# Router logits from extra columns of the attention's key and value matrices, score banks exponentiated from PSUM, and a large fill placed later

## The chip, the cores and the metric

The kernel runs on one core of one Trainium2 chip. The metric is the device time of one execution in microseconds (us). The kernel before was timed three times: 933.9, 938.02 and 944.68 us, median 938.02. Engines are named as in the profile: PE is TensorE (PEld its weight loads), DVE is VectorE, ACT is ScalarE, POOL is GpSimd, SP is SyncE, which here only starts DMAs.

## What is computed

A block with cross-attention and a mixture of nine experts, on 4 x 1024 tokens of 256 channels in float32. Layer norms, 16 heads of 64, 77 context rows per batch, two experts for each token:

```python
z = layernorm(layernorm(x)) ; c = layernorm(ctx)       # the second norm of each with weights and biases
q = (z @ Wq) * (1 + fside) + fside                     # 16 heads of 64
k, v = split(c @ Wkv)                                  # 77 rows for each batch
x = x + softmax(q @ k.T / 8) @ v @ Wout
h = layernorm(x)
logits = h @ Wr                                        # 9 experts; the top 2 of the softmax, weights w summing to 1
x = x + sum(w[e] * (silu(h @ Wg[e]) * (h @ Wu[e])) @ Wd[e] for e in top2)
```

The kernel never forms queries. For each batch it multiplies Wq into the keys (a *key matrix*, 256 x 16*77) and the values into Wout (a *value matrix*, 16*77 x 256). A token's scores are its normalised row times the key matrix, and the attention's output is its probabilities times the value matrix. Products that need full float32 accuracy are made from two float32r halves (hi, lo) in three matmuls (`product`, lines 224 to 231).

## The kernel before

**Stages.** Prepare (0 to about 74 us): the context is normalised, turned and multiplied by Wkv; Wq is mixed with the layer norm's weights; key and value matrices are made, and the value matrix goes through DRAM. Attention with routing (to about 389 us): T = 32 tiles of 128 tokens go through a software pipeline of T + 5 steps. Experts (408 us to the end): 40 tiles of 256 rows, gathered by expert, through gate, up and down products.

**The pipeline.** In step s, each engine runs its `step(s, c)`, an order written out by hand; engines meet only at semaphores. PE turns the probabilities of tile s-2 (line 996) in three groups, makes the router logits of tile s-4 (1020) from a transposed copy of the normalised row, makes the scores of tile s in three PSUM banks of 6, 6 and 4 heads, turns the next token rows (960) and the normalised rows of tile s-3 (964), makes the ranks of tile s-4 (1041, 1042), and multiplies probabilities by the value matrix (`attend`, tile s-2). DVE adds the attention of tile s-3 to the row, takes its statistics and normalises it, picks two experts for tile s-4 (`route`), inverts the sums of tile s-1 (`softmax_inv`), takes the minima of tile s and, for the first bank alone, subtracts them into SBUF (`softmax_in`, `DIRECT = 1`), and gives rows their slots (`allot`). ACT exponentiates the first bank of tile s-1 from SBUF and the other two of tile s straight from PSUM. POOL computes the reciprocal root of the variance, copies the row for the second expert (`make_rows`), multiplies the probabilities by the inverse sums (`divide`, 614), scatters two copies of the rows of tile s-5 to the experts' regions (`scatter`, 601, two indirect DMAs) and sums the gate's denominator of tile s-4 (`gate_sum`, 608). DVE's reciprocal of that sum (1352) is in its step between the probabilities' halves and `normalise`.

**Before the pipeline.** POOL fills `wq_head` (128 x 4096 elements, line 573) right after the root for the context's norm (572), while DVE normalises the context (1146). ACT later overwrites halves of `wq_head` with the mixed Wq. PE makes 8 pairs of key and value products, then the mixed Wq (929), then 32 key-matrix products (980) with 24 value products (947) between them.

## Time and profile before

| | us |
|---|---|
| median of three runs | 938.02 |
| the profiled execution's own time | 937.82 |
| its span, first to last instruction | 935.9 |
| prepare, until the first minimum of a score bank | 75.2 |
| attention and routing, until the ranks' last sum is read | 75.2 to 389.2 |
| gap until the experts' first matmul | to 408 |
| experts | 408 to 935.9 |
| PE, DVE, ACT, POOL busy | 865.1, 703.9, 650.7, 388.9 |

Busy times are sums over stages with different limits. Around the span lie 1.9 us in which no instruction runs. The chain of the work that ended last passes through PE for 67% of the span.

### The profile page before, as it was taken

What the parts mean: (1) busy time and instruction counts of PE and PEld (TensorE: products, weight loads), DVE (VectorE), ACT (ScalarE), POOL (GpSimd) and SP (SyncE); (2) the same over time, 40 slices, a digit from 0 to 9 for tenths busy, and PEclk for the clock granted to TensorE, in tenths of its full rate; (3) what the DMA queues carried; (4) which work ended last, traced back from release to release, by engine and by line L of the source; (5) the groups of instructions that cost most, each with busy time, mean ns of one, the idle gap of its engine ahead of it and who ended that gap; (6) DMA issues with size and microseconds to landing.
All of it is one profiled execution on the core that took longest, in us unless ns stands there. A gap on an engine that the chain in (4) does not pass through costs nothing.

```text
span 935.9 us, 22224 instructions
## 1 busy us (share of the span) xinstructions
PE 865.1 (92%) x6634; PEld 827.7 (88%) x6634; DVE 703.9 (75%) x1640; ACT 650.7 (70%) x2054; POOL 388.9 (42%) x475
## 2 busy tenths in 40 slices
PE   5997999999999998269999999999999999999993
PEld 4746999999999998259999999998999999999993
DVE  7766898888898786657876877776778777687771
ACT  3558888787888875247776777675767776677761
POOL 3001376676686666502343333333323433234332
PEclk9998999999999998769999999999999999999997
DMA  7158301310400207331225224355342254322222
GB/s 238 34 160 275 95 25 56 102 36 29 129 29 30 80 24 257 121 86 24 46 44 129 45 44 130 47 128 137 66 110 45 34 140 100 74 45 40 40 33 23
DMA packets 66681, 77.99 MB, mean 83 GB/s; under 512 B 7303, under 2 KB 58691, under 8 KB 66627
## 3 DMA queue, kind: packets, MB, share of 16 engines
q1 hardware_dynamic: 50947, 57.33, 20.6%
q0 software_dynamic: 14592, 18.95, 12.1%
q10 hardware_dynamic: 1088, 1.06, 0.4%
q8 instruction: 25, 0.41, 0.2%
q14 instruction: 29, 0.24, 0.1%
HBM read 113.46 MB, written 32.93 MB: 156 GB/s over the span
## 4 chain that ended last, share of the span: by engine, by line
PE 67%; DMA 11%; issue 7%; DVE 6%; SPq 4%; POOL 2%; ACT 2%; DVEq 1%; ACTq 0%; POOLq 0%
PE banks L229 19%; PE banks L230 18%; PE banks L231 18%; DMA wgt<-in_L_ffn_Wu 5%; PE banks L996 3%; DMA result<-res,tok_id 3%; PE banks L980 2%; PE banks L947 2%; PE banks L1099 1%; PE banks L1066 1%; PE banks L1020 1%; DVE hid_lo L1459 1%; DMA xs<-in_x 1%; POOL result L653 1%; PE banks L929 1%
## 5 line engine op out<-in xcount | busy, mean ns | idle before, releaser
L229 PE MATMUL banks<-tok_t_hi,wgt_hi 128*128 128x256 f32 x880 | 252.0, 286 | 9.6 <-DVE tok_t_lo L1428 9.5
L231 PE MATMUL banks<-tok_t_hi,wgt_lo 128*128 128x256 f32 x880 | 251.0, 285 | 0.0
L230 PE MATMUL banks<-tok_t_lo,wgt_hi 128*128 128x256 f32 x880 | 251.0, 285 | 0.0
L1440 DVE TENSOR_TENSOR wgt_lo<-wgt,wgt_hi 128x704 fp32r<-128x704 f32 (+1 forms) x240 | 207.6, 907 | 37.9 <-ACT wgt_hi L819 36.9
L653 POOL DMA_INDIRECT result<-res,tok_id x80 | 130.0, 1625 | 219.3 <-ACT res L846 191.5
L819 ACT ACTIVATE wgt_hi<-wgt 128x704 fp32r (+3 forms) x240 | 179.9, 800 | 31.2 <-DMA wgt<-in_L_ffn_Wu 24.5
L229 PEld LDWEIGHTS banks<-tok_t_hi,wgt_hi 128*128 128x128 f32 x880 | 171.0, 194 | 11.4 <-issue 11.3
L230 PEld LDWEIGHTS banks<-tok_t_lo,wgt_hi 128*128 128x128 f32 x880 | 171.1, 194 | 0.0
L231 PEld LDWEIGHTS banks<-tok_t_hi,wgt_lo 128*128 128x128 f32 x880 | 171.0, 194 | 0.0
L229 PE MATMUL banks<-wgt_hi,hid_hi 128*128 128x256 f32 x400 | 116.2, 290 | 0.0
L231 PE MATMUL banks<-wgt_hi,hid_lo 128*128 128x256 f32 x400 | 113.1, 283 | 0.0
L230 PE MATMUL banks<-wgt_lo,hid_hi 128*128 128x256 f32 x400 | 113.0, 283 | 0.0
L759 ACT ACTIVATE prob<-banks,row_min 128x77 f32<-128x77 f32 x320 | 98.8, 344 | 11.9 <-DVE row_min L1302 11.6
L614 POOL TENSOR_TENSOR prob<-prob,row_inv 128x1232 f32<-128x1232 f32 x32 | 72.1, 2253 | 60.0 <-DVE row_inv L1317 60.0
L229 PE MATMUL banks<-valmat_hi,prob_t_hi 128*128 128x256 f32 x320 | 94.3, 295 | 0.0
L230 PE MATMUL banks<-valmat_lo,prob_t_hi 128*128 128x256 f32 x320 | 91.7, 286 | 0.0
L231 PE MATMUL banks<-valmat_hi,prob_t_lo 128*128 128x256 f32 x320 | 91.6, 286 | 0.0
L644 POOL COPY tok_gate<-tok 128x2 f32<-128x2 f32 x40 | 22.2, 556 | 136.4 <-DMA result<-res,tok_id 124.0
L230 PEld LDWEIGHTS banks<-wgt_lo,hid_hi 128*128 128x128 f32 x400 | 76.6, 192 | 0.0
L229 PEld LDWEIGHTS banks<-wgt_hi,hid_hi 128*128 128x128 f32 x400 | 76.5, 191 | 0.0
L231 PEld LDWEIGHTS banks<-wgt_hi,hid_lo 128*128 128x128 f32 x400 | 76.5, 191 | 0.0
L601 POOL DMA_INDIRECT expert_in<-xn,top_slot x64 | 68.6, 1072 | 17.5 <-issue 16.6
(184 smaller groups left out, 2122.4 us busy)
## 6 DMA issues: line engine op xcount, KB each, us to landing
wgt<-in_L_ffn_Wg SPq DMA_DIRECT2D x40, 704.0 KB
wgt<-in_L_ffn_Wu SPq DMA_DIRECT2D x40, 640.0 KB
wgt<-in_L_ffn_Wd SPq DMA_DIRECT2D x40, 640.0 KB
...
```

The lines of the kernel that those rows point to most:

```text
L229: nc.tensor.matmul(to, a[0], b[0], start=first, stop=False)
L230: nc.tensor.matmul(to, a[0], b[1], start=False, stop=False)
L231: return nc.tensor.matmul(to, a[1], b[0], start=False, stop=last)
L601: nc.gpsimd.indirect_dma_start(expert_in, bass.IndirectOffsetOnAxis(ap=top_slot[c % 4][:, k:k + 1], axis=0), xn[c % 4][:, k, :], None).the ...
L614: nc.gpsimd.tensor_tensor(p, p, row_inv[i][:].unsqueeze(2).to_broadcast([P, H, M]), ALU.mult).then_inc(prob_ready, 1)
L644: nc.gpsimd.tensor_copy(tok_gate[i][:], tok[i][:, :, GATE])
L653: nc.gpsimd.indirect_dma_start(out, bass.IndirectOffsetOnAxis(ap=tok_id[i][:, a:a + 1], axis=0), res[i][:, a, :], None, compute_op=ALU.add ...
L759: ins = nc.scalar.activation(prob[c % 2][:, h * M:(h + 1) * M], bank[i][:, (h - h0) * M:(h - h0 + 1) * M], ACT.Exp, bias=row_min[c % 2][:, ...
L819: nc.scalar.activation(wgt_hi[i][:, p0:p1], loaded_weights(slot)[:, p0:p1], ACT.Copy).then_inc(weights_hi, 1)
L947: mm = nc.tensor.matmul(val_banks(m)[0:rows, i, :], v_t[half, c, r * P:r * P + rows], wout_sb[half, c, :], start=True, stop=True)
L996: mm = nc.tensor.transpose(bank[3 + (c * NG + g) % 2][0:n, (m - c0) * P:(m - c0 + 1) * P], prob[c % 2][:, m * P:m * P + n], ident[:])
L1440: nc.vector.tensor_tensor(wgt_lo[i][0:rows, p0:p1], loaded_weights(slot)[0:rows, p0:p1], wgt_hi[i][0:rows, p0:p1].bitcast(F32), ALU.subtra ...
```

## The change

- `wr_sb` gets one column of zeros (EX = 10 columns), the key matrix 10 columns behind the last head (the router's weights, split in hi and lo), the value matrix 10 columns Wout times Wr. So the third score bank holds 318 columns instead of 308, and the attention's output 266 instead of 256; `all_logits` puts the logits together from both, the row's mean and deviation. PE no longer turns the normalised rows (964) nor multiplies them by Wr (1020), and ACT no longer copies the turned rows (729). `gap` is scaled by the row's reciprocal deviation in ACT's exponential.
- For this, PE turns Wout in 16 transposes and makes Wout times Wr in 18 small matmuls before the value products.
- All three banks are exponentiated from PSUM; `softmax_in` goes. The third bank's exponentials stand in ACT's next step.
- Routing comes one step earlier: picks for tile s-3, slots and scatter for tile s-4, T + 4 steps in all. DVE's reciprocal for the gate is now first in its step, and `softmax_inv` stands behind the first minimum, `all_logits` and `allot`.
- POOL's fill of `wq_head` waits until DVE has split all of Wkv. DVE's preparation of `mix` stands between the fourth and fifth pair of keys.

```diff
             pool.wait_ge(ctx_stats, 1)
             nc.gpsimd.tensor_tensor(c_rstd[:], c_rstd[:], minus_half[:, 0:CR], ALU.pow).then_inc(ctx_rstd, 1)
+            pool.wait_ge(wkv_split, len(KV_PIECES))
             nc.gpsimd.memset(wq_head[:], 1.0 / D).then_inc(halves_filled, 1)
 
...
+                if has(s, 4):
+                    make_rows(s - 4, c - 4)
                 if has(s, 1):
                     divide(s - 1, (c - 1) % 2)
                 behind = s >= T
-                if behind and has(s, 4):
-                    gate_sum(s - 4, c - 4)
-                if has(s, 5):
-                    scatter(s - 5, c - 5)
-                if not behind and has(s, 4):
-                    gate_sum(s - 4, c - 4)
+                if behind and has(s, 3):
+                    gate_sum(s - 3, c - 3)
+                if has(s, 4):
+                    scatter(s - 4, c - 4)
+                if not behind and has(s, 3):
+                    gate_sum(s - 3, c - 3)
...
-            def softmax_exp(t, c, h0, h1):
-
-                act.wait_ge(scores_moved, (t + 1) * DIRECT)
+            def softmax_exp(t, c, i):
+
+                act.wait_ge(row_min_made, t * len(SCORE_BANKS) + i + 1)
+                h0, h1 = SCORE_BANKS[i]
...
+                    ins = nc.scalar.activation(prob[c % 2][:, h * M:(h + 1) * M], bank[i][:, (h - h0) * M:(h - h0 + 1) * M],
+                                               ACT.Exp, bias=row_min[c % 2][:, h:h + 1], scale=-1.0,
+                                               accum_out=row_sum[c % 2][:, h:h + 1])
+                ins.then_inc(exp_done, 1)
...
+                if has(s, 1):
+                    softmax_exp(s - 1, c - 1, 2)
                 if has(s, -1):
                     normed_plus_one(s + 1, (c + 1) % 2)
-                if has(s, 1):
-                    softmax_exp(s - 1, c - 1, 0, SCORE_BANKS[DIRECT][0]).then_inc(exp_done, 1)
+                if has(s, 0):
+                    softmax_exp(s, c, 0)
                 if has(s, 2):
                     prob_round(s - 2, c - 2, NG - 1)
-                if turns(s):
+                if has(s, -1):
                     turn_move(s, c)
+                if has(s, 0):
+                    softmax_exp(s, c, 1)
+                if has(s, 3):
+                    act.wait_ge(gap_ready, s - 2)
+                    act.wait_ge(y_rstd_made, s - 2)
+                    nc.scalar.activation(gap_exp[(c - 3) % 2][:], gap[(c - 3) % 2][:], ACT.Exp, scale=y_rstd[:]).then_inc(gap_exp_done, 1)
...
+            pe.wait_ge(wout_loaded, 16)
+            for n in range(4):
+                to = fill(PREP_OUT + n)
+                for c in range(4):
+                    at = n % 2 * 4 + c
+                    mm = nc.tensor.transpose(to[:, c * P:(c + 1) * P], wout_sb[:, at, n // 2 * P:(n // 2 + 1) * P], ident[:])
+                mm.then_inc(prep_made, 1)
+
...
+            to = fill(PREP_WR)
+            for c in range(PAIRS + 1):
+                for k in range(KT):
+                    w = wout_t[:, k, c * P:(c + 1) * P] if c < PAIRS else ones[:]
+                    mm = nc.tensor.matmul(to[:, c * EX:(c + 1) * EX], w, wr_sb[:, k, :], start=k == 0, stop=k == KT - 1)
+            mm.then_inc(prep_made, 1)
+
...
+                    mm = product(bank[i][:, 0:cols], [z[:, k, :] for z in zn_t[c % 2]],
+                                 [z[:, s // TB, at:at + cols] for z in keymat], k == 0, k == KT - 1)
...
+                    mm = product(bank[6][:, 0:DE], [p[0:n, m, :] for p in prob_t[c % 2]],
...
-                if has(s, 4):
-                    pe.wait_ge(turn_moved, s + 1)
-                    if c > 4:
-                        pe.wait_ge(slot_ready, s - 4)
-                    for k in range(KT):
-                        mm = nc.tensor.matmul(bank[7][:, 0:E], xn_t[c % 2][:, k, :], wr_sb[:, k, :],
-                                              start=k == 0, stop=k == KT - 1)
-                    mm.then_inc(logits_done, 1)
...
-                if has(s, 4):
-                    pe.wait_ge(picks_ready, s - 3)
-                    nc.tensor.matmul(bank[7][:, 16:16 + E], before[:], picks[:], start=True, stop=False)
-                    nc.tensor.matmul(bank[7][:, 16:16 + E], ones_h[:], picks_sum[:], start=False, stop=True
-                                     ).then_inc(ranks_done, 1)
...
+                if has(s, 3):
+                    pe.wait_ge(picks_ready, s - 2)
+                    nc.tensor.matmul(bank[7][:, 16:16 + E], before[:], picks[:], start=True, stop=False)
+                    nc.tensor.matmul(bank[7][:, 16:16 + E], ones_h[:], picks_sum[:], start=False, stop=True
+                                     ).then_inc(ranks_done, 1)
...
-            dve.wait_ge(consts_zero, 6)
+            dve.wait_ge(consts_zero, 7)
...
             for c in range(PAIRS):
+                if c == MIX_AT:
+                    mix_queries()
...
+            def own_logits(t, c):
+
+                h0, h1 = SCORE_BANKS[-1]
+                at = (h1 - h0) * M
+                dve.wait_ge(scores_done, (t + 1) * len(SCORE_BANKS))
+                nc.vector.scalar_tensor_tensor(out=x_logits[c % 4][:], in0=bank[len(SCORE_BANKS) - 1][:, at:at + E],
+                                               scalar=x_dev[:, t:t + 1], in1=x_lack[:, t, :], op0=ALU.mult, op1=ALU.subtract)
...
+                dve.wait_ge(exp_done, (t + 1) * len(SCORE_BANKS))
...
+            def all_logits(t, c):
+
+                settle()
+                nc.vector.scalar_tensor_tensor(out=centre[:], in0=wr_sum[:, 0:E], scalar=y_mv[:, 0:1], in1=x_logits[c % 4][:],
+                                               op0=ALU.mult, op1=ALU.subtract)
+                settle()
+                nc.vector.tensor_tensor(logits[:], bank[6][:, D:D + E], centre[:], ALU.subtract).then_inc(att_added, 1)
...
-                nc.vector.tensor_tensor(gap[c % 2][:], top8[:, 1:2], top8[:, 0:1], ALU.subtract).then_inc(gap_ready, 1)
+                nc.vector.tensor_scalar(gap[c % 2][:], top8[:, 1:2], top8[:, 0:1], None, ALU.subtract).then_inc(gap_ready, 1)
...
             def step(s, c):
+                if has(s, 4):
+                    dve.wait_ge(gate_den_made, s - 3)
+                    nc.vector.reciprocal(xn[(c - 4) % 4][:, 0, GATE:GATE + 1], gate_den[(c - 4) % 2][:]).then_inc(gate_made, 1)
                 if has(s, 3):
                     add_attention(s - 3)
                 if has(s, 2):
                     for g in range(NG - 1):
                         prob_rest(s - 2, c - 2, g)
-                if has(s, 5):
-                    dve.wait_ge(gate_den_made, s - 4)
-                    nc.vector.reciprocal(xn[(c - 5) % 4][:, 0, GATE:GATE + 1], gate_den[(c - 5) % 2][:]).then_inc(gate_made, 1)
+                if has(s, 0):
+                    softmax_min(s, c, 0)
+                if has(s, 3):
+                    all_logits(s - 3, c - 3)
+                if has(s, 4):
+                    allot(s - 4, c - 4)
+                if has(s, 1):
+                    softmax_inv(s - 1, c - 1)
+                if has(s, 0):
+                    softmax_min(s, c, 1)
+                    own_logits(s, c)
+                    softmax_min(s, c, 2)
+                if has(s, 3):
+                    top_two(c - 3)
+                if has(s, 2):
+                    prob_rest(s - 2, c - 2, NG - 1)
+                if has(s, -1):
+                    zn_rest(s, c)
                 if has(s, 3):
                     normalise(s - 3, c - 3)
-                if has(s, 4):
-                    route(s - 4, c - 4)
-                if has(s, 1):
-                    softmax_inv(s - 1, c - 1)
-                if has(s, 2):
-                    prob_rest(s - 2, c - 2, NG - 1)
-                if has(s, 0):
-                    softmax_min(s, c)
-                    softmax_in(s, c)
-                if has(s, -1):
-                    zn_rest(s, c)
-                if has(s, 4):
-                    allot(s - 4, c - 4)
+                    route()
```

How DVE's step changes, in the steady part (rows of one step; `gate_den` is the gate's denominator that POOL makes, `row_inv` the inverse sums that POOL's `divide` waits for). Before, from the step's first instruction to `row_inv`:

```order
L1285 TENSOR_TENSOR xs<-xs,banks 128x256 [waits att_done]
L1287 BN_STATS y_stats<-xs 128x6
L1289 BN_AGGR y_mv<-y_stats 128x2
L1278 TENSOR_TENSOR prob_t_lo<-banks,prob_t_hi 128x512 [waits prob_moved] x2
L1352 RECIPROCAL xn<-gate_den 128x1 [waits gate_den_made]
L1296 TENSOR_SCALAR xn<-xs,y_mv,y_rstd 128x256 [waits scattered0,y_rstd_made]
...
L1327 TENSOR_TENSOR gap<-top 128x1
L1329 TENSOR_TENSOR pick<-expert_ids,top_id 128x18
L1332 TENSOR_TENSOR picks<-pick 128x9
L1317 RECIPROCAL row_inv<-row_sum 128x16 [waits exp_done]
```

After, from the step's first instruction to `row_inv`:

```order
L1396 RECIPROCAL xn<-gate_den 128x1 [waits gate_den_made]
L1326 TENSOR_TENSOR xs<-xs,banks 128x256 [waits att_done]
L1328 BN_STATS y_stats<-xs 128x6
L1330 BN_AGGR y_mv<-y_stats 128x2
L1319 TENSOR_TENSOR prob_t_lo<-banks,prob_t_hi 128x512 [waits prob_moved] x2
L1344 TENSOR_REDUCE row_min<-banks 128x6 [waits scores_done]
L1362 SCALAR_TENSOR_TENSOR centre<-wr_sum,y_mv,x_logits 128x9
L1365 TENSOR_TENSOR logits<-banks,centre 128x9
L1386 TENSOR_TENSOR picked<-pick,banks 128x18 [waits ranks_done]
...
L1391 CAST top_slot<-slot_f 128x2
L1357 RECIPROCAL row_inv<-row_sum 128x16 [waits exp_done]
```

The reciprocal of `gate_den` went from behind the halves of the probabilities to the head of the step. Between it and `row_inv` stood normalising, picking and the logits' copy; now the addition, the statistics, the two halves, a minimum of a score bank, the logits and the slots stand there.

POOL's step keeps its order; only the tiles differ. After, from one `divide` (L628) to the next:

```order
L628 TENSOR_TENSOR prob<-prob,row_inv 128x1232 [waits inv_done]
L615 DMA expert_in<-xn,top_slot 41216x258 [waits rows_made,slot_ready]
L615 DMA expert_in<-xn,top_slot 41216x258
L622 TENSOR_TENSOR gate_den<-gap_exp,ones 128x1 [waits gap_exp_done]
L634 TENSOR_TENSOR y_var<-y_mv,eps 128x1 [waits y_stats_made]
L636 TENSOR_TENSOR y_rstd<-y_var,minus_half 128x1 [waits y_var_made]
L602 TENSOR_TENSOR xn<-gap_exp,xn 128x1 [waits gate_made]
L604 COPY xn<-xn 128x256
L605 COPY xn<-token_ids 128x2
L628 TENSOR_TENSOR prob<-prob,row_inv 128x1232 [waits inv_done]
```

The denominator (L622) stands behind `divide` and both scatters of its step, and DVE's reciprocal at the head of the next step waits for it (`gate_den_made`).

PE before the value products (L947 before, L976 after; `xs` holds Wout there, `mix` the mixed norm weights). Before:

```order
L231 MATMUL banks<-c_hi,wkv_lo 128x308
L929 MATMUL banks<-mix,wq_sb 128x256 [waits wr_loaded,prep_moved,wq_loaded,mix_made]
L929 MATMUL banks<-mix,wq_sb 128x256
...
L929 MATMUL banks<-mix,wq_sb 128x256
L947 MATMUL banks<-xs 128x256 [waits wout_loaded,prep_moved,keys_moved]
L947 MATMUL banks<-xs 128x256
L980 MATMUL banks<-k_head,wq_head 128x308
```

After:

```order
L944 MATMUL banks<-ident,xs 128x128 [waits prep_moved,wout_loaded]
L944 MATMUL banks<-ident,xs 128x128 x3
...
L944 MATMUL banks<-ident,xs 128x128 x3
L953 MATMUL banks<-mix,wq_sb 128x256 [waits wr_loaded,prep_moved,wq_loaded,mix_made]
L953 MATMUL banks<-mix,wq_sb 128x256
...
L953 MATMUL banks<-mix,wq_sb 128x256
L961 MATMUL banks<-wr_sb,wout_t 128x10 [waits prep_moved]
L961 MATMUL banks<-wr_sb,wout_t 128x10 x15
L961 MATMUL banks<-wr_sb,ones 128x10 x2
L976 MATMUL banks<-xs 128x266 [waits prep_moved,keys_moved]
```

Sixteen transposes of Wout went ahead of the mixed Wq, and 18 matmuls of 10 columns behind it; the first value product now waits for ACT's copy of their result (`prep_moved`).

## Rows read from the trace of the kernel before

**Rows 1.** Busy time in one stretch: us, then PE, PEld, DVE, ACT, POOL, clock, DMA
```profile
106.30:352.30 246.00, 245.59 (x1838) 236.34 (x1837) 209.29 (x756) 204.55 (x1096) 169.06 (x240) 1.00 0.16 52
```

**Rows 2.** Chain that ended last: start us, us, engine and line
```profile
106.30 0.88 PE banks L996 x8
...
352.29 0.88 PE banks L996 x8
```

**Rows 3.** Timeline of PE in one step: start us, us, what
```profile
143.44 0.51 PE L1020 MATMUL banks<-wr_sb,xn_t 128*128 128x9 f32 x4
143.81 0.46 PE L229 MATMUL banks<-keymat_hi,zn_t_hi 128*128 128x462 f32 x1
...
147.69 0.38 PE L964 MATMUL banks<-ident,xn 128*128 128x128 f32 x2
147.91 0.17 PE L1041 MATMUL banks<-picks,before 128*128 128x9 f16 x1
...
148.29 0.28 PE L231 MATMUL banks<-valmat_hi,prob_t_lo 128*128 128x256 f32 x1
148.40 0.28 PE L229 MATMUL banks<-valmat_hi,prob_t_hi 128*128 128x256 f32 x1
```

**Rows 4.** Timeline of DVE in the same step
```profile
142.77 0.42 DVE L1285 TENSOR_TENSOR xs<-xs,banks 128x256 f32<-128x256 f32 x1 [0.55 <-PE banks L231]
...
143.92 1.29 DVE L1278 TENSOR_TENSOR prob_t_lo<-banks,prob_t_hi 128x512 fp32r<-128x512 f32 x2
145.12 0.15 DVE L1352 RECIPROCAL xn<-gate_den 128x1 f32<-128x1 f32 x1
...
146.71 0.25 DVE L1317 RECIPROCAL row_inv<-row_sum 128x16 f32<-128x16 f32 x1
...
150.24 0.17 DVE L1337 TENSOR_TENSOR picked<-pick,banks 128x18 f32<-128x18 f32 x1
...
150.95 0.74 DVE L1208 BATCH_NORM_STATS2 x_stats<-xs 128x6 f32<-128x256 f32 x2
```

**Rows 5.** Timeline of POOL from that step's divide on
```profile
147.04 2.25 POOL L614 TENSOR_TENSOR prob<-prob,row_inv 128x1232 f32<-128x1232 f32 x1 [0.94 <-DVE row_inv L1317]
149.46 1.06 POOL L601 DMA_INDIRECT expert_in<-xn,top_slot  x1 [0.17 <-issue]
150.83 0.97 POOL L601 DMA_INDIRECT expert_in<-xn,top_slot  x1 [0.31 <-issue]
151.82 0.21 POOL L608 TENSOR_TENSOR gate_den<-gap_exp,ones 128x1 f32<-128x1 f32 x1
```

**Rows 6.** Groups by form, 115.4 to 352.3: busy us, mean ns, idle before
```profile
L1302 DVE TENSOR_REDUCE row_min<-banks 128x6 f32<-128x462 f32 x52 | 30.4, 625 | 0.0
...
L1296 DVE TENSOR_SCALAR xn<-xs,y_mv,y_rstd 128x256 f32<-128x256 f32 x26 | 10.3, 398 | 0.0
...
L601 POOL DMA_INDIRECT expert_in<-xn,top_slot x52 | 56.5, 1087 | 12.3 <-issue 12.3
```

**Rows 7.** Timeline of all engines at the context's normalisation
```profile
6.41 3.50 POOL L573 MEMSET wq_head<- 128x4096 f32 x1
6.48 4.22 DVE L1146 TENSOR_SCALAR c_sb<-c_sb,c_mv,c_rstd 128x256 f32<-128x256 f32 x3 [0.69 <-POOL c_rstd L572]
```

**Rows 8.** Chain in the preparation: the first value product
```profile
37.66 0.63 PE banks L947 x4
```

**Rows 9.** Timelines of POOL and DVE at the end of the pipeline
```profile
365.68 2.25 POOL L614 TENSOR_TENSOR prob<-prob,row_inv 128x1232 f32<-128x1232 f32 x1 [0.94 <-DVE row_inv L1317]
```
```profile
365.93 2.02 DVE L1338 TENSOR_TENSOR picks_sum<-picks_sum,picks 128x9 f16<-128x9 f16 x1
...
372.03 0.42 DVE L1285 TENSOR_TENSOR xs<-xs,banks 128x256 f32<-128x256 f32 x1 [3.60 <-PE banks L231]
...
380.01 0.42 DVE L1285 TENSOR_TENSOR xs<-xs,banks 128x256 f32<-128x256 f32 x1 [2.98 <-PE banks L231]
...
389.21 0.17 DVE L1386 COPY next_row<-banks 128x9 f32<-128x9 f32 x1 [0.22 <-PE banks L1058]
```

196 lines of the change are left out of this document (95 added, 101 removed).

## The prediction

> **What bounds the kernel now.** I read the busy time by stretch first, then the chain of the work that ended last, then the timelines of one step on each engine, to find what ends last in the stage that the change touches. From 106.3 to 352.3 us, the steady part of the pipeline, PE is busy for 245.6 of 246.0 us at full granted clock, DVE for 209.3, ACT for 204.6, POOL for 169.1 [rows 1]. The chain runs over PE with the same line at the head of each step: step 4 begins at 106.30, step 31 at 352.29, so 27 steps take 245.99 us, 9.11 each [rows 2]. The others have slack on average, but each executes its step in order, and a loop through several engines can be longer than the busy time of any of them. So beside PE's sum I add up the loops that the new order closes.
>
> **PE's step gets lighter.** The logits' four passes go: 143.44 to 143.81, 0.37 us; the two transposes of the normalised rows go: 147.69 to 147.91, 0.22 us [rows 3]. Against that stand 10 more columns in 30 matmuls of the attention and 6 of the scores. A matmul of 256 columns follows its predecessor by 0.11 to 0.12 us [rows 3], so 10 columns cost at most 0.005, and 36 of them 0.17 us. PE would need 9.11 - 0.59 + 0.17 = 8.69 us a step. Were PE still the bound, 28 steps would give back 12 us.
>
> **A loop through DVE and POOL gets longer.** In a step POOL waits for the inverse sums (`row_inv`), multiplies, issues two scatters and only then sums the gate's denominator. From `row_inv` at 146.71 to the end of that sum (151.82 + 0.21) it takes 5.32 us: 2.25 of it the multiplication, then 1.37 and 0.99 for the scatters with the time between them [rows 4, 5]. Before, DVE needs the denominator only at 145.12, behind the two halves of the probabilities, and `row_inv` follows 1.59 us later [rows 4]: the loop is 5.32 + 1.59 = 6.9 us, 2.2 less than a step, and hidden behind PE. After, the reciprocal of the denominator is the first thing in DVE's step, and all of this stands between it and `row_inv`:
> - the reciprocal 0.07 (an undrained small operation), the addition and statistics 1.15 (142.77 to 143.92), the two halves 1.20 (143.92 to 145.12) [rows 4];
> - the first minimum 0.63 [rows 6] and about 0.10 for the drain behind it;
> - two small operations of `all_logits`, 0.24 with the drain between them and 0.08. The 0.24 is worked out from `allot`: 0.71 us from 150.24 to 150.95 for four small operations of which two are drained, the plain ones 0.07 and 0.16 [rows 4];
> - `allot`, 0.71.
>
> That is 4.18 us. A semaphore from DVE to POOL takes 0.08 (146.96 to 147.04) [rows 4, 5]; I take the same for the way back. The loop is then 5.32 + 0.08 + 4.18 = 9.58 us, longer than PE's 8.69 and than today's 9.11. It closes once per step from step 4 to step 32, 28 times. The scatters average 1.09 us against 1.06 and 0.97 in this step [rows 6], so I take 9.65. Bounds: 9.4 if the new small operations overlap better, 10.0 if each scatter is delayed by what DVE does beside it. I expect 28 x (9.65 - 9.11) = **+15 us** (+8 to +25). What is late next: PE waits some 0.5 us for `att_added`, which now comes behind `all_logits`, and 0.4 for the picks, which stand behind `attend`; DVE waits about 1 us for the denominator. Taking `softmax_in` away and exponentiating all banks from PSUM lies in that slack: ACT's load is 204.6 of 246 [rows 1], it loses the copy of the turned rows, and neither engine is in the loop. The third bank's exponentials in ACT's next step come before `row_inv` is due; the wait that they add lies behind nothing that PE needs.
>
> **The preparation.** The fill of `wq_head` and DVE's normalisation run together: 3.50 us from 6.41, and three operations that take 4.22 us from 6.48 [rows 7], where the same form takes 0.40 elsewhere [rows 6]. They end 0.8 us after the fill. With the fill gone they should take about 1.1 us: -3.1. The Trainium skill ("SBUF — State Buffer", Who interferes with whom) says that a VectorE instruction in a 2-port mode and a GpSimd instruction exclude each other for their whole length; the row agrees with it. The fill now waits for DVE's last split of Wkv and meets DVE's small operations there; if it blocks them, the keys' scaling starts up to 3 us later, as late as today. PE waits for it only from its fifth pair on; I put 0 to 1 us on PE. PE gains new work on its path: 16 transposes at 0.11 (0.88 for 8 [rows 2]), 1.8 us, and 18 matmuls with two passes each at 0.09 (0.37 for four [rows 3]), 3.2 us, then some 0.7 for ACT's copies before the first value product, which today starts right behind the mixed Wq at 37.66 [rows 8]. With 24 value products 10 columns wider, 0.4, and half of that 1 us: 1.8 + 3.2 + 0.7 + 0.4 + 0.5 - 3.1 = **+3.5 us** (+2.5 to +5; +6.6 if the fill was not the cause). In step 1, `row_inv` of tile 0 moves behind a minimum: **+0.6** [rows 6].
>
> **The end.** From the last addition of attention, 380.01, to the reading of the ranks, 389.21, 9.2 us pass today, with the logits' transposes, copies and products of two tiles in them [rows 9]. After, that addition is followed by: addition and statistics 1.0, the last aggregate 0.3, `all_logits` 0.3, `allot` 0.7, picking 0.5, normalising 0.4, the two steps to `picks` 0.5, PE 0.4, `allot` 0.8, PE and the read 0.4: 5.3 us, 3.9 less. The addition before it stands at 372.03, 7.98 us earlier [rows 9], and PE's attention of the last tile is held in between by turned rows and picks. After, it waits for the halves (2.4 from the addition on), `all_logits` (0.4) and its own 3.8: 6.7, so 1.3 less, and I take the same for the step before that. Together 3.9 + 1.3 + 1.3: **-6.5 us** (-3 to -8). What follows, the tail stores, is untouched and starts earlier by as much.
>
> **Sum.** The profiled execution's own time is 937.8 us, at the median of the runs, 938.0. 937.8 + 15.1 + 3.5 + 0.6 - 6.5 = 950.5; I say **951 us**. With the bounds of its terms this case reaches from 943 to 961.
>
> **Rivals.**
> - *PE stays the bound.* The loop would have to be under 8.7 us, so that POOL or DVE parts of it overlap in a way that the rows do not show. For it: PE is busy all the time now [rows 1]. Against it: every link is a semaphore or program order. 28 x (8.69 - 9.11) = -11.8, and 937.8 - 11.8 + 3.5 + 0.6 - 6.5 = 924. Chance 0.12. This one ends on the other side; it decides as soon as the loop is under 9.05.
> - *The loop is partly hidden*, 9.15 to 9.35 a step, or the end gives back more than I say: +1 to +7 for the steps, 937 to 944. Chance 0.14.
> - *The gap is blocked.* DVE's `gap` is now a TENSOR_SCALAR and falls into POOL's multiplication. An SBUF operation of DVE was held there at the end of the pipeline: `picks_sum` took 2.02 us beside the multiplication that began 0.25 us before it [rows 9], against a drained pitch of 0.24. Held from about 1.8 us after `row_inv` until POOL is done at 2.6, DVE loses 0.75. From `row_inv` to the next step it has about 4.4 us of work (two minima 1.1, picking 0.9, two halves 0.8, normalising 0.4, `picks` 0.5, statistics 0.7) and 5.4 to do it in, so that only the two steps in each of three batches with variances, offsets and `val_rest` overrun, by some 0.6 each: +4, 955. Chance 0.12. That section of the Trainium skill's page on SBUF gives this result if the one-element operation runs in a 2-port mode.
> - *PE's new pauses cost it the clock.* It is granted 1.00 now [rows 1]; if the gaps of 0.9 us a step made it fall, the attention's 30 matmuls would double and overrun the slack by 1.9 us a step: over 1000. Chance 0.03.
> - *The fill is not the cause* of the 4.22 us: +3.1, 954; chance 0.05, and it adds to any other.
>
> My forecast has 0.54. About 1% (9.4 us) is what a measurement of this kernel can tell from no change. Of the forecast's 943 to 961, some five parts in six lie over 947.4; with the gap, the clock and the fill, slower by over 1% has 0.62. The partly hidden loop, the rest of the forecast and a small part of the first rival make 0.26 within 1%. PE as the bound leaves 0.12. The range leaves out that rival and the clock: 937 to 961.
>
> **What would show it.** Right: PE's step pitch is 9.5 to 9.8; on DVE, the gate's reciprocal stands behind idle time of about 1 us released by POOL's `gate_den`, and PE idles before `attend` and before the ranks, released by DVE. The three normalisations take about 1.1 us, the first value product starts near 41, and the last addition is 5 to 6 us before the ranks' read. Wrong: a pitch of 8.7 with no wait for `gate_den`; or a wait elsewhere in DVE's step, such as `gap` or `val_rest` lengthened beside POOL's multiplication; or PE at less than its full granted clock between 110 and 370 us.

## Result, and the profile after

The changed kernel takes 956.04 us (median of 4 runs, 955.1 to 956.85) against 936.74 for the kernel before (median of 4, 933.9 to 944.68): a ratio of 1.021, 95% interval 1.017 to 1.025. The profiled execution's own time is 955.1 us, 17.3 more than the 937.8 of before. The change makes the kernel slower by some 2%.

The two traces can be laid side by side at points that both have: the first minimum of tile 0, the attention's additions on DVE (one per step, from step 3 on), and the copy that reads the last ranks.

| from ... to | before | after | difference | forecast |
|---|---|---|---|---|
| start to the first minimum (preparation) | 75.24 | 84.82 | +9.6 | +3.5 |
| first minimum to the addition of step 3 | 22.58 | 26.43 | +3.8 | +0.6 |
| addition of step 3 to that of step 4 | 8.51 | 8.44 | -0.1 | 0 |
| addition of step 4 to that of step 32 | 254.85 | 268.45 | +13.6 | +15.1 |
| addition of step 32 to the ranks' read | 28.03 | 20.98 | -7.0 | -6.5 |
| ranks' read to the end (own time) | 548.6 | 546.0 | -2.6 | 0 |
| sum | 937.8 | 955.1 | +17.3 | +12.7 |

The last stretch, -2.6, is not counted as an effect of the change. It is the same code in all kernels below, and between the ranks' read and the end of the span it took from 540.9 to 547.5 us in the fourteen profiled executions of this study (546.7 before, 543.8 after).

The rows of the steady part come first. The timeline of DVE in the changed kernel (start us, us, line, operation) shows that the gate's reciprocal, L1396, is now the first operation of the step and that DVE stood idle before it:

```profile
152.71 0.25 DVE L1357 RECIPROCAL row_inv<-row_sum 128x16 f32<-128x16 f32 x1
...
154.46 0.19 DVE L1373 TENSOR_SCALAR gap<-top 128x1 f32<-128x1 f32 x1
...
158.16 0.16 DVE L1396 RECIPROCAL xn<-gate_den 128x1 f32<-128x1 f32 x1 [1.23 <-issue]
158.24 0.40 DVE L1326 TENSOR_TENSOR xs<-xs,banks 128x256 f32<-128x256 f32 x1
...
162.23 0.24 DVE L1357 RECIPROCAL row_inv<-row_sum 128x16 f32<-128x16 f32 x1
```

And the timeline of POOL between these two `row_inv`:

```profile
153.04 2.25 POOL L628 TENSOR_TENSOR prob<-prob,row_inv 128x1232 f32<-128x1232 f32 x1 [1.62 <-DVE row_inv L1357]
155.46 1.17 POOL L615 DMA_INDIRECT expert_in<-xn,top_slot  x1 [0.17 <-issue]
156.94 0.97 POOL L615 DMA_INDIRECT expert_in<-xn,top_slot  x1 [0.30 <-issue]
157.93 0.20 POOL L622 TENSOR_TENSOR gate_den<-gap_exp,ones 128x1 f32<-128x1 f32 x1
```

From `row_inv` (152.71) to the end of the denominator's sum (158.13) 5.42 us pass, 0.03 more to the reciprocal, and 4.07 from there to the next `row_inv`: 9.52 us, and nothing in the circle waits for anything outside it. Before, the same points were 5.32 us apart on POOL's side and had 2.2 us to spare [rows 4, 5]. The waits of DVE from 120 to 370 us (line; waited for; us in total, times, longest) put most of the idle time before L1396 down to "issue", since POOL's sum, which is what the reciprocal waits for in the program, ends only 0.03 us ahead of it:

```profile
DVE xn L1396 <- issue: 21.9, 17, 1.9
DVE xn L1396 <- POOL gate_den L622: 3.9, 3, 1.3
```

A kernel with the same pipeline (the one with the narrow matmuls first, below) has the same waits of 1.3 us under POOL's name:

```profile
DVE xn L1398 <- POOL gate_den L622: 23.8, 19, 1.9
```

In the preparation, two things are new. The timeline of PE, from the transposes of Wout to the first value product:

```profile
28.89 1.91 PE L944 MATMUL banks<-ident,xs 128*128 128x128 f32 x16
30.64 7.07 PE L953 MATMUL banks<-mix,wq_sb 128*128 128x256 f32 x32
37.55 3.64 PE L961 MATMUL banks<-wr_sb,wout_t 128*128 128x10 f32 x32
41.04 0.59 PE L961 MATMUL banks<-wr_sb,ones 128*128 128x10 f32 x4
42.12 0.76 PE L976 MATMUL banks<-xs 64*128 64x266 f32 x4 [0.49 <-ACT wr_sum L728]
```

Then the busy time by stretch (stretch; its length; busy us of PE, PEld, DVE, ACT, POOL; granted clock; DMA share; GB/s). The granted clock falls to half, 1.2 of 2.4 GHz, within a microsecond behind that wait, and stays there to about 53 us (in this execution):

```profile
41.00:42.00 1.00, 0.63 (x6) 0.54 (x5) 0.00 (x0) 0.33 (x4) 0.00 (x0) 1.00 0.00 0
42.00:43.00 1.00, 0.88 (x5) 0.52 (x6) 0.00 (x0) 0.30 (x3) 0.00 (x0) 0.83 0.00 0
43.00:44.00 1.00, 1.00 (x2) 0.31 (x2) 0.00 (x0) 0.53 (x1) 0.00 (x0) 0.50 0.00 0
...
50.00:52.00 2.00, 2.00 (x6) 0.75 (x6) 1.26 (x3) 0.22 (x1) 0.00 (x0) 0.50 0.19 62
52.00:54.00 2.00, 2.00 (x10) 0.54 (x6) 0.48 (x1) 1.19 (x3) 0.00 (x0) 0.77 0.71 186
```

In the kernel before the clock was 1.00 from 36 to 58 us.

Behind the first minimum, DVE waits for a load that the change does not touch, the second part of x, with `row_inv` of tile 0 queued behind:

```profile
95.33 0.76 DVE L1230 BATCH_NORM_STATS2 x_stats<-xs 128x6 f32<-128x256 f32 x2 [7.16 <-DMA xs<-in_x]
...
96.54 0.24 DVE L1357 RECIPROCAL row_inv<-row_sum 128x16 f32<-128x16 f32 x1
```

The kernel before has the same wait, but shorter:

```profile
84.06 0.75 DVE L1208 BATCH_NORM_STATS2 x_stats<-xs 128x6 f32<-128x256 f32 x2 [5.24 <-DMA xs<-in_x]
84.73 0.23 DVE L1317 RECIPROCAL row_inv<-row_sum 128x16 f32<-128x16 f32 x1
```

### The profile page after: what moved, and what is told of

Read it like the earlier page. It is cut to its first block, busy times and chain, and to the rows that moved or that the text cites. A ratio compares the mean times of both kernels' runs of the same rounds, so it can differ in the third digit from the quotient of the medians.

```text
span 952.9 us, 22005 instructions
## 1 busy us (share of the span) xinstructions
PE 873.2 (92%) x6494; PEld 812.5 (85%) x6494; DVE 697.9 (73%) x1686; ACT 655.0 (69%) x2030; POOL 384.1 (40%) x476
## 4 chain that ended last, share of the span: by engine, by line
PE 41%; DVE 16%; issue 13%; DMA 11%; ACT 5%; POOL 5%; SPq 4%; DVEq 4%; ACTq 0%; POOLq 0%
PE banks L238 11%; PE banks L239 11%; PE banks L240 11%; DMA wgt<-in_L_ffn_Wu 5%; DVEq L1142 4%; DMA result<-res,tok_id 3%; ACT prob L772 3%; DVE row_min L1344 2%; DVE prob_t_lo L1319 2%; PE banks L1003 2%; POOL expert_in L615 2%; PE banks L976 2%; DVE y_stats L1328 1%; PE banks L1115 1%; PE banks L1082 1%
## 5 line engine op out<-in xcount | busy, mean ns | idle before, releaser
L772 ACT ACTIVATE prob<-banks,row_min 128x77 f32<-128x77 f32 x512 | 159.0, 343 | 43.5 <-DVE row_min L1344 43.5
L772 ACT ACTIVATION_READ_ACCUMULATOR prob<-banks,row_min 128x1 f32 x512 | 115.1, 225 | 0.0
L628 POOL TENSOR_TENSOR prob<-prob,row_inv 128x1232 f32<-128x1232 f32 x32 | 72.1, 2252 | 80.4 <-DVE row_inv L1357 80.4
L238 PE MATMUL banks<-valmat_hi,prob_t_hi 128*128 128x266 f32 x320 | 96.4, 301 | 6.2 <-DVE logits L1365 5.4
L239 PE MATMUL banks<-valmat_lo,prob_t_hi 128*128 128x266 f32 x320 | 92.3, 288 | 0.0
L240 PE MATMUL banks<-valmat_hi,prob_t_lo 128*128 128x266 f32 x320 | 92.0, 287 | 0.0
L658 POOL COPY tok_gate<-tok 128x2 f32<-128x2 f32 x40 | 24.5, 613 | 137.7 <-DMA result<-res,tok_id 124.1
```

The lines of the kernel that those rows point to most:

```text
L238: nc.tensor.matmul(to, a[0], b[0], start=first, stop=False)
L239: nc.tensor.matmul(to, a[0], b[1], start=False, stop=False)
L240: return nc.tensor.matmul(to, a[1], b[0], start=False, stop=last)
L628: nc.gpsimd.tensor_tensor(p, p, row_inv[i][:].unsqueeze(2).to_broadcast([P, H, M]), ALU.mult).then_inc(prob_ready, 1)
L658: nc.gpsimd.tensor_copy(tok_gate[i][:], tok[i][:, :, GATE])
L772: ins = nc.scalar.activation(prob[c % 2][:, h * M:(h + 1) * M], bank[i][:, (h - h0) * M:(h - h0 + 1) * M], ACT.Exp, bias=row_min[c % 2][:, ...
```

## Experiments

"Step" is always the mean distance of DVE's additions from step 4 to step 32: 9.10 us before, 9.59 after. Each median is compared with the kernel before as it was timed in the same session; the medians of two changed kernels mostly come from different sessions, and the kernel before itself has medians from 933.79 to 937.47 in them.

### What makes the step longer

The first edit puts DVE's reciprocal back behind the halves and leaves all else of the change in.

```diff
             def step(s, c):
-                if has(s, 4):
-                    dve.wait_ge(gate_den_made, s - 3)
-                    nc.vector.reciprocal(xn[(c - 4) % 4][:, 0, GATE:GATE + 1], gate_den[(c - 4) % 2][:]).then_inc(gate_made, 1)
                 if has(s, 3):
                     add_attention(s - 3)
                 if has(s, 2):
                     for g in range(NG - 1):
                         prob_rest(s - 2, c - 2, g)
+                if has(s, 4):
+                    dve.wait_ge(gate_den_made, s - 3)
+                    nc.vector.reciprocal(xn[(c - 4) % 4][:, 0, GATE:GATE + 1], gate_den[(c - 4) % 2][:]).then_inc(gate_made, 1)
```

> The changed kernel with one edit: VectorE's reciprocal of the gate's denominator stands behind the two halves of the probabilities again, as in the kernel before. My theory (the loop of the row reciprocal, the division, two scatters, the sum, the gate's reciprocal, the addition, the statistics, the halves, the logits and the next row reciprocal sets the step of 9.59 us): 4.08 us of that loop ran between the row reciprocal and the gate's reciprocal, and here the halves run meanwhile, so TensorE's own work of about 8.7 us is the step again; 28 steps by 0.8 to 0.9 give 22 to 25 us, about 931 to 934. Rival (something else in the step, such as the three exponentials or TensorE's waits on the halves, sets the 9.59): the step stays at 9.4 or more and the time at 952 to 956.

Measured: 933.65 us (928.76 to 938.2, 10 runs), ratio to the kernel before 0.998 (0.9945 to 1.0015). The step is 8.77 us. PE is busy for 252.11 of the 255 us from 106 to 361. The same stretch of DVE's timeline:

```profile
139.37 0.41 DVE L1326 TENSOR_TENSOR xs<-xs,banks 128x256 f32<-128x256 f32 x1
...
141.63 0.15 DVE L1401 RECIPROCAL xn<-gate_den 128x1 f32<-128x1 f32 x1
...
143.43 0.24 DVE L1357 RECIPROCAL row_inv<-row_sum 128x16 f32<-128x16 f32 x1
```

And POOL's sum in the same step:

```profile
139.28 0.22 POOL L622 TENSOR_TENSOR gate_den<-gap_exp,ones 128x1 f32<-128x1 f32 x1
```

POOL's sum of the denominator ends at 139.50 there, 0.13 us behind the start of the addition. In the changed kernel the addition would have waited for it; here it does not, and the denominator has 2.1 us to spare.

The step of 8.77 is 0.33 us shorter than that of the kernel before, so the extra columns do relieve PE, by 9 us in 28 steps. The time is hardly shorter all the same: the addition of step 3 comes at 111.78 us, 14 us later than before (97.82), which uses up these 9 us and most of the 7 that the end of the pipeline gives back.

The second edit leaves the reciprocal first in the step and shortens the other side of the circle, POOL's.

```diff
-                behind = s >= T
+                behind = True
                 if behind and has(s, 3):
                     gate_sum(s - 3, c - 3)
                 if has(s, 4):
                     scatter(s - 4, c - 4)
```

> The changed kernel with one edit on GpSimd: the sum of the gate's denominators stands ahead of the two scatters in every step, not only in the last ones. My theory: the two scatters (1.2 and 1.0 us, 2.2 together) leave the loop, so it takes about 9.6 - 2.2 = 7.4 us, less than TensorE's 8.7; the step falls to about 8.7 and the time to 931 to 934, the same as with the reciprocal moved. Rival (GpSimd itself is the bound, or the loop is another one): the step stays at 9.4 or more and the time within 4 us of 956.

Measured: 934.12 us (930.0 to 937.27, 10 runs), ratio 0.9987 (0.9955 to 1.0018), step 8.82. Either edit opens the circle, one on each engine. The rival that something else sets the 9.59 has fallen. POOL and DVE in a step of this kernel:

```profile
135.45 2.25 POOL L628 TENSOR_TENSOR prob<-prob,row_inv 128x1232 f32<-128x1232 f32 x1
137.66 0.24 POOL L622 TENSOR_TENSOR gate_den<-gap_exp,ones 128x1 f32<-128x1 f32 x1
138.35 1.07 POOL L615 DMA_INDIRECT expert_in<-xn,top_slot  x1 [0.46 <-issue]
```

```profile
135.73 0.19 DVE L1373 TENSOR_SCALAR gap<-top 128x1 f32<-128x1 f32 x1
...
136.57 1.28 DVE L1337 TENSOR_SCALAR xn<-xs,y_mv,y_rstd 128x256 f32<-128x256 f32 x1
...
140.13 0.15 DVE L1396 RECIPROCAL xn<-gate_den 128x1 f32<-128x1 f32 x1
```

The sum is done at 137.90, 2.2 us before the reciprocal wants it.

The third edit does the one thing alone, in the kernel before: the reciprocal goes from behind the halves to the head of the step, and nothing else changes.

```diff
             def step(s, c):
+                if has(s, 5):
+                    dve.wait_ge(gate_den_made, s - 4)
+                    nc.vector.reciprocal(xn[(c - 5) % 4][:, 0, GATE:GATE + 1], gate_den[(c - 5) % 2][:]).then_inc(gate_made, 1)
                 if has(s, 3):
                     add_attention(s - 3)
...
                     for g in range(NG - 1):
                         prob_rest(s - 2, c - 2, g)
-                if has(s, 5):
-                    dve.wait_ge(gate_den_made, s - 4)
-                    nc.vector.reciprocal(xn[(c - 5) % 4][:, 0, GATE:GATE + 1], gate_den[(c - 5) % 2][:]).then_inc(gate_made, 1)
```

> The kernel before with one edit of the change alone: the gate's reciprocal stands at the head of VectorE's step. My theory: with the two exponentiated banks as they were, the loop through GpSimd is closed all the same and takes 5.3 (the kernel before, row reciprocal to sum) + 0.1 + about 4.0 for the addition, statistics and halves ahead of the row reciprocal = 9.4 us against 9.10 now, so 28 by 0.3 = 8 us more, about 945. Rival (the place of the reciprocal alone costs nothing, it takes the third bank's exponential a step later to close the loop): 936 to 938.

Measured: 947.87 us (943.78 to 951.49, 4 runs), ratio 1.012 (1.005 to 1.020), step 9.56. The waits of DVE from 120 to 370 us, in 24 of the steps (the step grows by 0.46 us, where I expected 0.3):

```profile
DVE xn L1347 <- POOL gate_den L608: 28.4, 24, 1.6
```

So the place of one small operation costs 0.46 us a step in the kernel before (9.56 against 9.10) and 0.81 in the changed one (268.45 against 245.66 us in 28 steps). The two closed circles are of about one length, 9.56 and 9.59; the cost differs by what the step would be without them. To close the circle takes neither the exponentials of all banks from PSUM nor their lateness.

### What makes the preparation longer

The next edit moves the narrow matmuls (Wout times Wr, 18 of 10 columns, two passes each, which the trace counts as 36) and ScalarE's copies of their result ahead of the mixed query products. The cut shows the order of the banks; PE's and ScalarE's instructions move with it.

```diff
-        PREP_WQ = PREP_OUT + 4
-        PREP_WR = PREP_WQ + PAIRS
-        PREP = PREP_WR + 1
+        PREP_WR = PREP_OUT + 4
+        PREP_WQ = PREP_WR + 1
+        PREP = PREP_WQ + PAIRS
```

> The changed kernel with one edit in the preparation: the product of the output matrix with the router's (36 matmuls of 10 columns) and ScalarE's copies of it stand ahead of the four mixed query products and not right ahead of the value products. Theory: the granted clock fell to 0.50 from 42.8 to 52.9 us because TensorE had done narrow matmuls for 3.9 us and then waited 0.5 us for ScalarE; with four products of 512 columns and more between, the clock stays 1.00 at the start of the value products, and these end 5 us earlier; with the wait for ScalarE gone 5 to 6 us less in all, 950 to 951. Rival (the clock falls for the whole amount of work since the transposes, whatever the order, or the fall has nothing to do with it): a stretch of 0.50 of about 10 us still there, and 954 to 957.

Measured: 957.97 us (956.8 to 959.97, 4 runs), ratio 1.025 (1.018 to 1.032). Nothing is gained. The fall has moved with the narrow matmuls, which now begin at 31.70, behind a wait of 0.89 us (PE is busy for 0.30 of the stretch from 31 to 32):

```profile
31.00:32.00 1.00, 0.30 (x3) 0.33 (x3) 0.97 (x3) 0.60 (x2) 0.00 (x0) 1.00 0.00 0
...
33.00:34.00 1.00, 1.00 (x10) 1.00 (x9) 0.97 (x3) 0.00 (x0) 0.00 (x0) 0.86 0.00 0
34.00:35.00 1.00, 1.00 (x7) 1.00 (x6) 0.95 (x3) 0.00 (x0) 0.00 (x0) 0.50 0.00 0
...
40.00:41.00 1.00, 1.00 (x5) 0.85 (x4) 0.00 (x0) 0.45 (x2) 0.00 (x0) 0.72 0.00 0
```

The fall goes with the narrow matmuls, not with the value products or the amount of work done by 42 us. My expectation that order alone would cure it was wrong.

Next the narrow matmuls are spread between the mixed products (two pairs behind each of products 1 to 4, the column sums behind product 5), in a bank that the keys have left. The base is the kernel with the late reciprocal. The cut shows PE's new loop; a wait for the fifth pair of keys, whose bank it uses, stands ahead of the mixed products, and ScalarE's copies of the narrow products move ahead of its copy of mixed product 6.

```diff
+                if c == 1:
+                    pe.wait_ge(prep_moved, PREP_WQ)
+                for p in range(2 * (c - 1), min(2 * c, PAIRS + 1)) if c else ():
+                    for k in range(KT):
+                        w = wout_t[:, k, p * P:(p + 1) * P] if p < PAIRS else ones[:]
+                        mm = nc.tensor.matmul(bank[4][:, p * EX:(p + 1) * EX], w, wr_sb[:, k, :], start=k == 0, stop=k == KT - 1)
+                    if p == PAIRS:
+                        mm.then_inc(prep_made, 1)
```

> The kernel with the late gate's reciprocal (933.65) with the narrow products of the output matrix and the router's spread between the mixed query products, two pairs behind each of products 1 to 4 and the column sums behind product 5, in a bank of their own, so that ScalarE's copies of them end before the last mixed products. The run with these products moved whole ahead of the mixed ones had its fall of the granted clock right behind their start (0.86 in 33 to 34 us, 0.50 to 40 us), so the fall follows the narrow products. Theory A (36 of them in a row bring the fall, or they with the 0.5 us wait behind them): spread out, the clock stays 1.00 and the wait for ScalarE is gone, 5 to 6 us less, 927 to 929. Rival B (any 36 such products bring it): a stretch of 0.50 of about 10 us still there, 931 to 934.

Measured: 930.47 us (926.87 to 935.45, 10 runs), ratio to the kernel before 0.994 (0.9906 to 0.9974). The clock stays at 1.00, though PE waits longer than before, 0.95 us, for ScalarE:

```profile
41.00:42.00 1.00, 0.73 (x4) 0.30 (x2) 0.00 (x0) 0.89 (x3) 0.00 (x0) 1.00 0.00 0
42.00:43.00 1.00, 0.32 (x3) 0.33 (x4) 0.00 (x0) 0.89 (x4) 0.00 (x0) 1.00 0.00 0
43.00:44.00 1.00, 1.00 (x6) 0.30 (x2) 0.00 (x0) 0.57 (x1) 0.00 (x0) 1.00 0.00 0
```

The first value product starts at 42.68, 0.5 us later than in the base, since ScalarE's copies of the mixed products have become the last thing. The first minimum is at 81.00 against 84.86 all the same, 3.9 us earlier, and from the first value product to the first minimum it takes 38.32 us against 42.66: the low clock cost 4.3 us. In the median the gain over the base is not resolved: the two ratios to the kernel before, 0.994 and 0.998, have intervals that overlap.

Two causes are still mixed in that: the narrow ones are no longer in a row, and wider products stand between them and the wait. The next kernel has them in a row again, behind product 5, with products 6 and 7 between them and the wait; the loop's range and the place of PE's wait for the turned Wout tell it from the one before.

```diff
-                if c == 1:
+                if c == 5:
                     pe.wait_ge(prep_moved, PREP_WQ)
-                for p in range(2 * (c - 1), min(2 * c, PAIRS + 1)) if c else ():
+                for p in range(PAIRS + 1) if c == 5 else ():
```

> The kernel with the narrow products spread (930.5) with all 36 of them in a row again, behind the mixed product 5 and ahead of products 6 and 7, so that 36 narrow ones in a row stand there with no wait of TensorE behind them and 16 wider matmuls after. In the spread kernel a wait of 0.95 us (41.7 to 42.7 us) brought no fall. If the row of narrow ones alone brings the fall: a stretch of 0.50 within some 5 us of their start, first minimum at about 85 us (81.0 spread), about 933. If it takes the row and the wait behind it together: the clock stays 1.00 here and the first minimum at 81.

Measured: 928.83 us (928.55 to 933.52, 4 runs), ratio 0.996 (0.992 to 1.000). In the profiled execution the row runs from 35.66 to 39.6, the clock stays at 1.00, and the first minimum is at 81.00. Taken alone, this spoke for the row and the wait together. But the trace of the kernel with the sum first speaks against it: there the fall begins within the row, ahead of any wait. Its row of narrow passes runs from 38.09 to 42.6, and the first wait ends at 43.08:

```profile
40.00:41.00 1.00, 1.00 (x11) 1.00 (x11) 0.00 (x0) 0.00 (x0) 0.00 (x0) 1.00 0.00 0
41.00:42.00 1.00, 1.00 (x9) 1.00 (x9) 0.00 (x0) 0.00 (x0) 0.00 (x0) 0.79 0.00 0
```

So one more kernel has the row two products earlier, far from the wait (`c == 3` in place of `c == 5`, with ScalarE's copies moved ahead of product 4).

> The row of 36 narrow passes two products earlier, behind the mixed product 3, so that products 4 to 7 (16 passes of 256 columns) stand between it and ScalarE's wait. What speaks against the wait as a condition: in the kernel with the sum first the granted clock was already 0.67 at 41.5 us, within the row (38.1 to 42.6), and the wait came only behind it. If the row alone can bring the fall, with its moment or not from execution to execution: a stretch of 0.50 beginning within 5 us of the row's start (some 33.7) and a first minimum at 83 to 85 us; if this execution is again without it (first minimum 81), both kernels with wider products between row and wait go without, and the case for the products around the row is stronger, though not closed.

Measured: 931.52 us (929.64 to 936.29, 4 runs), ratio 0.997 (0.990 to 1.003), first minimum at 84.47. The fall is back, three microseconds into the row, with PE busy all the time before it:

```profile
33.94 4.17 PE L967 MATMUL banks<-wr_sb,wout_t 128*128 128x10 f32 x32
37.95 1.01 PE L967 MATMUL banks<-wr_sb,ones 128*128 128x10 f32 x4
38.80 6.11 PE L959 MATMUL banks<-mix,wq_sb 128*128 128x256 f32 x16
```

```profile
36.00:37.00 1.00, 1.00 (x11) 1.00 (x10) 0.05 (x1) 0.00 (x0) 0.00 (x0) 0.93 0.00 0
37.00:38.00 1.00, 1.00 (x7) 1.00 (x6) 0.00 (x0) 0.00 (x0) 0.00 (x0) 0.50 0.00 0
```

So the row can bring the fall with no wait at either end; the first minimum is 3.5 us later than with the row behind product 5. The fall began between 2.0 and 5.1 us behind the start of the row in seven of the eight profiled executions that have one (the changed kernel and six experiments), three times within the row and four times behind it, and in the eighth, with the row behind product 5, not at all. Spread, there was none, in one profiled kernel and in the one with all edits; the four profiled kernels without narrow products have none either. What decides the moment, and why one execution was spared, stays open, and with one row in eight spared, two spread executions do not prove that spreading always helps. All of this rests on profiled executions: the ratios with the row behind products 5 and 3, 0.996 and 0.997, do not tell the two kernels apart.

The fill is tested from both sides. In the changed kernel it is held a little longer:

```diff
-            pool.wait_ge(wkv_split, len(KV_PIECES))
+            pool.wait_ge(keys_moved, 1)
             nc.gpsimd.memset(wq_head[:], 1.0 / D).then_inc(halves_filled, 1)
```

> The changed kernel with its large fill held until the first key product is moved, some 4 us later than now. In the changed kernel the fill (15.15 us, 3.57 us long) lies on VectorE's scaling of the side factors, which took 3.59 us for 128x64 values. Theory (the fill stops that instruction, and this costs little since TensorE's key and value products have their own pace): it takes under 0.3 us here, the key products begin earlier by up to 3 us, but the first value product only by 0 to 1.5; 954 to 957. Rival (those 3.5 us are the missing part of the preparation): 951 to 953.

and in the kernel before it gets the wait that the change gives it:

```diff
+            pool.wait_ge(wkv_split, len(KV_PIECES))
             nc.gpsimd.memset(wq_head[:], 1.0 / D).then_inc(halves_filled, 1)
```

> The kernel before with the move of the fill alone. Theory: the three normalisations of the context take 1.05 us in all in place of 4.22 and the preparation gains up to 3 us, of which the scaling of the side factors, now under the fill, takes back what TensorE's products do not cover: 0 to 3 us less, 933 to 937. Rival (the gain is all given back): the first key-matrix product where it is in the kernel before, and no change.

Measured: 952.56 us (950.93 to 956.41, 4 runs), ratio to the kernel before 1.019 (1.013 to 1.025), for the first, 938.37 (933.98 to 941.26, 10 runs) with a ratio of 1.0018 (0.999 to 1.0045) for the second. In the changed kernel, DVE's and POOL's rows are these:

```profile
6.47 1.05 DVE L1162 TENSOR_SCALAR c_sb<-c_sb,c_mv,c_rstd 128x256 f32<-128x256 f32 x3 [0.60 <-POOL c_rstd L585]
...
15.18 3.59 DVE L1190 TENSOR_SCALAR side_shift<-side 128x64 f32<-128x64 f32 x1
```

```profile
15.15 3.57 POOL L587 MEMSET wq_head<- 128x4096 f32 x1 [8.71 <-DVE wkv_lo L1171]
```

With the fill held back in it, and then in the kernel before with the fill moved:

```profile
15.24 0.18 DVE L1190 TENSOR_SCALAR side_shift<-side 128x64 f32<-128x64 f32 x1
```

```profile
15.46 3.59 DVE L1175 TENSOR_SCALAR side_shift<-side 128x64 f32<-128x64 f32 x1
```

The three normalisations fall from 4.22 to 1.05 us [rows 7], and the scaling of 64 values takes all of this back, 3.59 us in place of 0.18. In the kernel before, the first value product then starts at 38.04, not at 37.59 (by the same timeline), and the first minimum is at 75.69 against 75.24: no gain at all, which is what the rival of that expectation said. Held until behind the scaling, the fill costs the keys nothing and the first value product comes 1.2 us earlier (40.92 against 42.12). The first minimum comes 4.1 us earlier (80.72), because the fall of the clock was also shorter in that execution (0.50 for 3.4 us, from 41.0 to 44.4, against 10.2 us). Its median is 3.5 us below the changed kernel's, from another session, and lies where I had put the rival that those 3.5 us are missing from the preparation; the first value product gives only 1.2 of them. How much of the rest would come again is open.

### What makes the start of the pipeline later

The load of x for batch 1 is issued right behind the last store of the values, ahead of the wait for the stores and of the values' load. Base: the kernel with the late reciprocal.

```diff
+            load_x(1)
             for n in range(STORES, STORES + STORE_BUFFERS):
                 sp.wait_ge(val_stored[n % STORE_BUFFERS], stored_before(n))
...
             load_valmat(0)
-            load_x(1)
```

> The kernel with the late gate's reciprocal (933.65) with the load of x of batch 1 issued right behind the last store of the values and not behind the load of the values. In its trace VectorE stands 7.66 us idle before the first token statistics of batch 1 (95.88 us) until that load lands, with the minimum of tile 1 and the row reciprocal of tile 0 behind them; in the kernel before the same wait is 5.24 us. Theory: ScalarE's last exponential of tile 0 ends at 90.8, so the row reciprocal of tile 0 comes at about 91.2 in place of 97.1, and the time falls by 5 to 6 us, to 928 to 929. Rival (the values of batch 0, now landing later behind x, take the place of the wait): no gain, 932 to 936.

Measured: 926.01 us (924.77 to 929.77, 4 runs), ratio to the kernel before 0.990 (0.984 to 0.995), 2 us below what I expected. The first minimum stays at 84.76. Then:

```profile
89.11 0.75 DVE L1230 BATCH_NORM_STATS2 x_stats<-xs 128x6 f32<-128x256 f32 x2 [1.00 <-DMA xs<-in_x]
...
90.76 0.25 DVE L1357 RECIPROCAL row_inv<-row_sum 128x16 f32<-128x16 f32 x1 [0.35 <-ACT prob L772]
```

`row_inv` of tile 0 comes 6.3 us earlier than in the base (97.09), the addition of step 3 is at 107.02 against 111.78. From the first minimum to that addition it is now 22.26 us, against 26.92 in the base and 22.58 before. So this load accounts for the whole +3.8 us of the start.

The same edit in the kernel before:

> The kernel before with the load of x of batch 1 issued right behind the last store of the values: what this edit, which the change doesn't hold, is worth without the change. Its wait before the first token statistics of batch 1 is 5.24 us (until 84.06); the exponentials of tile 0 end before it. If the start is set by that wait: 4 to 5 us less, 932 to 933. If the second tile's own work (its statistics, at 90.3, and row reciprocal at 92.6, behind ScalarE) follows at its old time: 1 to 2 us less or none, 935 to 937.

Measured: 934.0 us (930.54 to 937.27, 10 runs), ratio 1.000 (0.998 to 1.002). No gain is measured, the least that the second case of the expectation allows. In the profiled execution `row_inv` gains 2.2 us (84.73 to 82.49) and the addition of step 3 2.7 us (97.82 to 95.17), of which 1.3 is left at the ranks' read. `row_inv` waits for ScalarE instead:

```profile
82.49 0.25 DVE L1317 RECIPROCAL row_inv<-row_sum 128x16 f32<-128x16 f32 x1 [3.33 <-ACT prob L750]
```

In the kernel before, tile 0's exponentials ended only 1.1 us ahead of the load (82.95 and 84.06). In the changed one they end earlier in the step, 6.0 us behind the first minimum in place of 7.7, and the load comes 11 us later, so the load alone sets the start.

### All of it together

The last kernel has the late reciprocal, the spread narrow products, the early load and the late fill.

> The changed kernel with all the edits that helped or might: the gate's reciprocal behind the halves, the narrow products spread, the load of x of batch 1 ahead, the fill held until the first key product is moved. If the gains add up from the single runs (late reciprocal 933.65; spread products -3.2; early load -7.6; fill -1.2 by its first value product): 921 to 924, faster than both kernels by more than 1%. If the early load and the spread products give back the same wait (values of batch 0 landing later than both): 925 to 928.

Measured: 925.7 us (921.71 to 927.14, 4 runs), ratio to the kernel before 0.990, 95% interval 0.987 to 0.993. It is faster than both kernels, by 8 us against 933.79 in the same session. The addition of step 3 is at 101.94, 9.8 us earlier than with the late reciprocal alone, about the sum of the parts (3.3 + 4.8 + 1.2). The step is 8.78. The median misses the 921 to 924 of gains that add up. It lies in the range that I gave to the rival, that two edits give back the same wait, and it is no better than that of the kernel with the early load alone (926.01, another session). Yet in the traces the gains do add up at step 3, where this kernel is 5.1 us ahead of that one; 3.2 of them are left at the ranks' read. Neither account of the median is settled, and that the two extra edits pay in it is not shown.

## Why the prediction was right, and where its steps were off

The forecast, 951 us with 937 to 961, held the measured 956.04, and "slower by over 1%" came true, by the mechanism named. That the sum came out so near is in part luck: the preparation left its bounds and the start was 3 us over, and 2.6 us of the expert phase, which no term foresaw, made up for some of it. By its steps:

- **PE's step gets lighter**: right. With the circle opened the step is 8.77 us, where I had 8.69 for PE alone, and PE is busy for all but 1%. PE's waits in the changed kernel are smaller than I said: 3.4 us for the logits and 0.8 for the picks from 120 to 370 us, some 26 steps, where I had 0.5 and 0.4 us in each.
- **The loop through DVE and POOL**: right in kind and nearly in size. 5.42 + 0.03 + 4.07 = 9.52 us in the rows, 9.58 forecast; mean step 9.59 against the 9.65 taken, +13.6 us against +15.1. The parts were off both ways: POOL's side took 5.42 in place of 5.32 us, the 0.10 of it from one scatter's start to the next (1.48 in place of 1.37), and DVE's side with the semaphore 4.10 in place of 4.26. The mark-up of 0.07 was for slower scatters, and they were no slower (1.07 us on average against the 1.09 of [rows 6]); the mean is 0.07 above the 9.52 because of a few longer steps (up to 10.1 us), several of them with a split of the next batch's value matrix in DVE's step (L1310, 0.98 us). Three experiments show it: opened on DVE's side, opened on POOL's side, and closed alone in the kernel before.
- **The preparation**: +9.6 measured, +3.5 forecast, outside its own bounds up to +6.6. Two terms failed. The fill's -3.1 + 0.5: I saw that the moved fill would meet DVE's small operations and even that the keys might be "as late as today", yet charged PE only 0.5 of it; by the run with the fill's move alone the two together are +0.4. And the clock: I asked what PE's waits in the pipeline would do to it and not what the new row of narrow matmuls would do in the preparation. That was 4.3 us. Of the other terms, the 16 transposes (1.75, forecast 1.8) and ScalarE's copies (0.49, forecast 0.7) stood up, and two were too small: 36 narrow passes took 4.1 (3.2, at 0.113 each in place of 0.09), and from the first value product to the first minimum it takes 38.3 to 38.6 us in the kernels with wider value products that have the full clock there, 0.7 to 1.0 more than the 37.65 before, where I had 0.4. Against that, PE began its transposes at 28.89, 1.7 us ahead of where the kernel before began the mixed products (30.59). A move that I had not priced can explain this, the mix of the queries behind the first keys; no run has it alone.
- **`row_inv` of tile 0, +0.6**: a mis-sized term, +3.8. The minimum ahead of it was not what cost the time: DVE's statistics in the same step wait for a load, and a preparation that ends later issues this load later. I priced the moved operation and put the load at nothing; with the load early the stretch takes 22.26 us, less than the 22.58 before.
- **The end, -6.5**: -7.0 measured. From the last addition to the ranks' read 5.54 us (5.3 forecast).
- **Rivals.** PE as the bound and the partly hidden loop fell with the step of 9.59. The blocked `gap` fell: it takes 0.19 us within POOL's multiplication, as the row at 154.46 shows. The clock in the pipeline stayed at 1.00; the fall came elsewhere. That the fill was not the cause of the 4.22 us fell with the 1.05.

The forecast was 5 us low. By the table, the misses are +6.1 in the preparation and +3.2 at the start, against -1.5 in the loop, -0.5 at the end and -2.6 in the expert phase.
